# Issuing the attention inner loop of a transformer layer by pairs of key tiles, with a fourth score bank

## The reference

```python
xn = _layernorm(x)                       # x: (8, 2048, 1024)
# attention branch
c_q, c_kv = xn @ W_DQ + b_DQ, xn @ W_DKV + b_DKV          # 32 wide
q = concat([c_q @ W_UQ + b_UQ, c_q @ W_QR + b_QR])        # per head 128 + 32
k = concat([c_kv @ W_UK + b_UK, xn @ W_KR + b_KR])        # the 32-wide part is shared by the heads
v = c_kv @ W_UV + b_UV                                    # per head 128
attn = softmax(q @ k.T / sqrt(160)) @ v                   # per head, 2048 x 2048
out_a = attn @ W_O + b_O
# expert branch: gates from a few rounds of normalisation, best two of eight
g, p = relu(xn @ wg[e]), xn @ wp[e]
out_f = sum over the two best e of gate[e] * ((g * p) @ wo[e])
return x + out_a + (xn + out_f)
```

## Time and profile before

| | us |
|---|---|
| median of 3 runs | 3950.96 |
| lowest run | 3939.86 |
| the profiled execution | 3941.66 |
| its span on the slowest core (core 1) | 3940.1 |
| spans of the 8 cores | 3915.8 to 3940.1 |

### The profile page before, as it was taken

The page is one execution under the profiler, slowest core; times in us unless marked ns, Lnnn a source line. Parts: engine busy times, 40 slices in busy tenths (PEclk is TensorE's granted clock), DMA queues, the critical chain, the costliest instruction groups (busy, mean ns, idle before and its releaser), DMA issues.

```text
span 3940.1 us, 43697 instructions; the slowest of 8 cores (3915.8 to 3940.1 us)
## 1 busy us (share of the span) xinstructions
PE 3601.7 (91%) x15210; PEld 1463.8 (37%) x15210; DVE 830.0 (21%) x1274; ACT 745.0 (19%) x1211; POOL 726.7 (18%) x1038
## 2 busy tenths in 40 slices
PE   3599999999999999898989899999999999999997
PEld 1243444444344444222222222444444444444443
DVE  3321121212121121122222222212121111212121
ACT  2310101101010101244444443011010101011010
POOL 1022222222222222000000000122222222222221
PEclk8699999999999999788888879999999999999998
DMA  4178879797878879300000000487878879787876
GB/s 75 37 74 107 92 95 110 76 114 73 113 76 112 95 92 110 52 1 0 1 1 0 1 1 1 79 110 79 119 67 110 83 105 100 87 110 78 118 67 131
DMA packets 618328, 290.68 MB, mean 74 GB/s; under 512 B 547324, under 2 KB 547357, under 8 KB 618118
## 3 DMA queue, kind: packets, MB, share of 16 engines
q0 software_dynamic: 610624, 271.03, 58.9%
q1 hardware_dynamic: 7494, 16.86, 1.3%
HBM read 550.39 MB, written 8.39 MB: 142 GB/s over the span
## 4 chain that ended last, share of the span: by engine, by line
PE 84%; DVE 5%; DMA 4%; ACT 3%; issue 3%; POOL 0%; DVEq 0%; SPq 0%; ACTq 0%; POOLq 0%
PE psum L625 22%; PE psum L557 21%; PE psum L565 21%; PE psum L788 4%; PE psum L784 4%; DMA s_areaC<-wexp 3%; DVE s_resid L647 3%; PE psum L774 3%; PE psum L778 3%; PE psum L819 2%; PE psum L676 1%; ACT s_areaB L794 1%; PE psum L358 1%; ACT s_areaB L726 1%; ACT s_areaB L719 1%
## 5 line engine op out<-in xcount | busy, mean ns | idle before, releaser
L625 PE MATMUL psum<-s_areaC,s_areaA 128*128 128x512 bf16 x4096 | 944.4, 391 | 102.8 <-DVE s_resid L647 73.7
L557 PE MATMUL psum<-s_xnT,s_wgbuf 128*128 128x512 bf16 x4096 | 967.6, 379 | 20.5 <-DVE s_resid L647 16.4
L565 PE MATMUL psum<-s_xnT,s_wpbuf 128*128 128x512 bf16 x4096 | 967.6, 379 | 0.0
L576 ACT ACTIVATE s_areaB<-psum 128x512 bf16<-128x512 f32 x512 | 306.2, 598 | 2458.1 <-PE psum L557 2457.8
L521 POOL DMA_DIRECT2D s_wgbuf<-wg x256 | 224.6, 877 | 2285.0 <-PE psum L557 2213.9
L625 PEld LDWEIGHTS psum<-s_areaC,s_areaA 128*128 128x128 bf16 x4096 | 406.8, 100 | 637.8 <-issue 191.5
L583 DVE TENSOR_TENSOR s_areaA<-s_areaB,psum 128x512 bf16<-128x512 bf16 x512 | 352.2, 688 | 1351.6 <-PE psum L565 1345.7
L557 PEld LDWEIGHTS psum<-s_xnT,s_wgbuf 128*128 128x128 bf16 x4096 | 399.0, 98 | 506.8 <-issue 28.5
L565 PEld LDWEIGHTS psum<-s_xnT,s_wpbuf 128*128 128x128 bf16 x4096 | 400.8, 98 | 483.3
L606 POOL DMA_DIRECT2D s_areaC<-wexp x512 | 271.9, 539 | 678.9 <-PE psum L625 677.2
L647 DVE SCALAR_TENSOR_TENSOR s_resid<-psum,s_w_tm,s_resid 128x512 f32<-128x512 f32 x256 | 192.1, 750 | 935.4 <-PE psum L625 911.4
(11 more groups left out here) (113 smaller groups left out, 706.5 us busy)
## 6 DMA issues: line engine op xcount, KB each, us to landing
s_areaC<-wexp POOLq DMA_DIRECT2D x512, 256.0 KB, 7.9
s_wgbuf<-wg POOLq DMA_DIRECT2D x256, 256.0 KB, 4.6
s_wpbuf<-wp POOLq DMA_DIRECT2D x256, 256.0 KB, 5.7
s_resid<-x SPq DMA_DIRECT2D x16, 512.0 KB, 3.8
y<-s_resid SPq DMA_DIRECT2D x2, 4096.0 KB, 12.6
s_areaC<-wo_attn POOLq DMA_DIRECT2D x1, 2048.0 KB, 14.1
s_wcat<-wdq POOLq DMA_DIRECT2D x1, 64.0 KB, 4.0
s_wcat<-wdkv POOLq DMA_DIRECT2D x1, 64.0 KB, 4.1
```

The costliest lines, as they stand in the source:

```text
L557: w.do("tensor", lambda t, c_=c, tb_=tb, tt2_=tt2, gs_=gs, b_=gb: t.matmul(bank(b_)[:, :], S["wgbuf"].ap()[:, gs_, c_, :], S["xnT"].ap()[: ...
L565: w.do("tensor", lambda t, c_=c, tb_=tb, tt2_=tt2, gs_=gs, b_=pbk: t.matmul(bank(b_)[:, :], S["wpbuf"].ap()[:, gs_, c_, :], S["xnT"].ap()[ ...
L576: w.do("scalar", lambda s, b_=gb, sl_=gp_count % 2: s.activation(out=Ebuf[:, sl_, :], in_=bank(b_)[:, :], func=AF.Relu), inc="sS")
L625: w.do("tensor", lambda t, f_=f, dh_=dh, tt_=tt, bk_=bk, ws_=ws, tb_=tb: t.matmul(bank(bk_)[:, :], hbuf[:, f_, tt_ * 128:(tt_ + 1) * 128], ...
```

## The change

The iteration of the inner loop covers two key tiles. Iteration `t_` waits for the exponential of tile `2 t_ - 2` (the newer of the two whose output comes next is `k0 = 2 t_ - 2`, the older is `k1 = 2 t_ - 3`), issues O and Z of `k1`, O and Z of `k0`, and then S1 and S2 of the tiles `2 t_` and `2 t_ + 1`. There are 10 iterations instead of 18. The scores rotate over four banks, 0, 1, 4 and 5. Bank 4 is therefore no longer free for the broadcast of the reciprocal, which now goes into the bank of the sum it was made from (3 or 7), and no longer waits for the earlier copy out of bank 4. The broadcast is issued after iteration 3, which is after S2 of tile 7. `Ebuf` keeps its three slots.

```diff
-                h_, qb_, qg_, ob_, rectok = pend
+                h_, qb_, qg_, ob_, zb_, rectok = pend
                 w.wait("tensor", "vS", rectok)
-                w.wait("tensor", "vS", tok.get("przb_cp"))
-                w.do("tensor", lambda t: t.matmul(bank(4)[:, :], S["onesr"][:], rzv,
-                                                  start=True, stop=True), inc="tS")
+                w.do("tensor", lambda t, zb2=zb_: t.matmul(bank(zb2)[:, :], S["onesr"][:], rzv,
+                                                           start=True, stop=True), inc="tS")
...
-                w.do("vector", lambda v: v.tensor_copy(rzbv, bank(4)[:, :]), inc="vS")
+                w.do("vector", lambda v, zb2=zb_: v.tensor_copy(rzbv, bank(zb2)[:, :]), inc="vS")
...
-                    for kt in range(NT + 2):
-                        ko = kt - 2
-                        if ko >= 0:
-                            w.wait("tensor", "sS", tok[("exp_s", h, qb, ko)])
-                        if kt == 0:
+                    for t_ in range(NT // 2 + 2):
+                        k1, k0 = 2 * t_ - 3, 2 * t_ - 2
+                        if k0 >= 0:
+                            w.wait("tensor", "sS", tok[("exp_s", h, qb, min(k0, NT - 1))])
+                        if t_ == 0:
...
-                        if ko >= 0:
-                            (O and Z of tile ko)
-                        if kt < NT:
-                            b = (0, 1, 5)[kt % 3]
+                        for ko in (k1, k0):
+                            if 0 <= ko < NT:
+                                (O and Z of tile ko)
+                        for kt in (2 * t_, 2 * t_ + 1):
+                            if kt >= NT:
+                                continue
+                            b = (0, 1, 4, 5)[kt % 4]
                             (S1, S2 and the exponential of tile kt)
...
-                        if kt == 5:
+                        if t_ == 3:
                             flush_przb()
...
-                    tok["pend"] = (h, qb, qg, ob, w.tok("vS"))
+                    tok["pend"] = (h, qb, qg, ob, zb, w.tok("vS"))
```

More of the change, by code:

```diff
@@ L772, in walk @@
                             w.wait("tensor", "sS", tok.get("exp_prev_last"))
-                        if ko >= 0:
[L774 to L781, removed]
-                        if kt < NT:
-                            b = (0, 1, 5)[kt % 3]
+                        for ko in (k1, k0):
+                            if 0 <= ko < NT:
+                                w.do("tensor", lambda t, kt_=ko, ob_=ob: t.matmul(
+                                    bank(ob_)[:, :], v_h[:, kt_, :], Ebuf[:, kt_ % 3, :],
+                                    start=(kt_ == 0), stop=(kt_ == NT - 1)),
+                                    inc="tS" if ko == NT - 1 else None)
+                                w.do("tensor", lambda t, kt_=ko, zb_=zb: t.matmul(
+                                    bank(zb_)[:, :], S["onesm"][:], Ebuf[:, kt_ % 3, :],
+                                    start=(kt_ == 0), stop=(kt_ == NT - 1)),
+                                    inc="tS" if ko == NT - 1 else None)
+                        for kt in (2 * t_, 2 * t_ + 1):
+                            if kt >= NT:
+                                continue
+                            b = (0, 1, 4, 5)[kt % 4]
                             w.do("tensor", lambda t, kt_=kt, b_=b, qb_=qb: t.matmul(
```

## The result

The changed kernel takes 4010.8 us (median of 9 runs) against 3949.3 us for the kernel before (median of 10 runs): the ratio is 1.0165, with a 95% interval of 1.0146 to 1.0183. It is slower by 1.65%, or some 65 us by the ratio (the two medians lie 61.5 us apart), which is inside the 2% that the chances spoke of, and clear of the measurement's own noise. Forecast were 4003 us, with 3972 to 4035 as the range. Some executions of any 8-core kernel here are disturbed and much longer; all ratios in this document, and all means over several executions, leave them out, while the medians do not.

A forecast was written before the change was run, and what follows sets the result against it. The prediction took TensorE's own stream to set the time, with ScalarE hidden. It summed 3941.7 us (profiled execution) + 58 (blocks) + 2 (half clock) = 4002, rounded up to 4003 us; range 3972 to 4035.

The forecast's parts named there:

- The balance before: Old attention inner loop: O starts 1.30 us after its own S2, just covering the 1.29 us needed, almost no slack.
- The stall: Changed inner loop at full clock: TensorE waits 0.42 us per pair for the newer exponential; pair 2.55 us against 2.14.
- The block: Attention query block of 16 tiles at full clock: 19.31 us before, 21.12 after; +1.81 us over 32 blocks, +58 us.
- The half clock: Start of attention heads at 1.2 GHz: 142 us costing 63 before, 181 us costing 65 after, +2 us.
- The parts at nothing: Attention's four score banks, broadcast into the finished sum's bank, dropped wait and later VectorE oT copy: no cost.
- The sum: Whole kernel: profiled execution 3941.7 us plus 58 and 2 gives 4002, rounded up to 4003 us.
- rival 1: Clock falls again inside attention heads, in three blocks of four: +112 us, 4115 us, slower by over 2%; chance 0.10.
- Rival 2: Clock returns at 5 us in every attention head: -49 instead of +2, 3951 us, no change; chance 0.05.
- Rival 3: No wait in the attention pair, 2.13 us each; only the end-of-block wait changes, -13 us, 3929 us; chance 0.02.

The follow-up runs named there:

- the last run: Kernel before plus trimmed unread matmuls (384 columns in projections, extra ones before attention and after each head's last value projection), run once more: ratio 0.9893, median 3906.3 us.
- the first form: Unread 512-column matmuls added in the projections: kernel before 0.9939, changed kernel 1.0091, changed kernel with split wait 0.9939, all against the kernel before.
- the trimmed form: Unread matmuls cut to 384 columns after 512-wide projections, extra ones before attention and after value projections: split wait 0.9884 and 0.9874, old loop 0.9879 and 0.9893.

## Why the prediction was right

**The balance before: right.** The 1.29 us from S2 to its own O, against 1.30 us that the old order gave it, was the number on which the rest hung. The shorter exponential shows both sides of it: with 0.21 us less on ScalarE, the kernel before loses 10 us (13 expected from the blocks' ends), and the pair of the changed one follows one to one.

**The stall: right in place and size.** 2.55 us a pair was forecast and measured, 1.28 against 1.29 us for the release. Splitting the wait removed it, with everything else of the change in place.

**The block: 0.06 us too low.** 19.31 and 21.12 us were forecast, 1.81 apart. At clock 1.00 throughout, a head gives 77.2 / 4 = 19.3 and 84.7 / 4 = 21.2 us, 1.88 apart, so 60 us instead of 58. The interval Z to O, for which no row existed, was 0.21 us as taken (1916.35 to 1916.56). What is left is rounding: O to Z and Z to O are 0.215 us, so that the pair is 2.56, six times a block, and the tail 1.39 instead of 1.36.

**The half clock: the weakest step, and the sum of it came out near by luck.** I gave the two heads with early returns the 25 us of their neighbours and kept the other six, 181 us in all; it was 161 us on the slowest core. The reasoning that the early returns at 5 us would be lost was right in that no head of the changed kernel returned before 6 us after its start. But the returns did not gather at 25 us: they came after 7 to 8, 12, 16, 24, 30 or 34 us. The price of 0.36 us for a half-clock microsecond holds: a head with 33 us lasts 97.0 us and one at full clock 84.7, 0.37 each, and over the eight heads (735 us, about 679 at full clock) it is 0.35. The price before, 0.44, was a little high: the eight heads of core 1 last 678.5 us in the kernel before and 619.4 at full clock in the last run, 59 us for 142, or 0.42 each. So the term was 161 x 0.35 = 56, against 59 before: -3 instead of +2. That the changed loop has more half clock is shown by the executions on record (494 us a core against 471), and the prediction had that direction right. Which heads return late differs from kernel to kernel and between cores with the same code, and no experiment here settles what decides it: the kernel with the shorter exponential has 78 us on two cores and 213 on a third.

**The parts at nothing: right.** Banks and broadcast alone gave 1.0002. VectorE's later copy held up nothing: the list of waits of the changed kernel in attention has none of O or Z for VectorE.

**The sum** was 3941.7 + 60, rounded up to +61; by the ratio the change is +65, and between the two profiled executions +67. With the terms as measured, the blocks give +60 and the half clock -3, 57 in all, and the stretch forecast grew by 57.6. That the forecast of 4003 is so near 4010.8 is in part luck: the blocks' 2 us too few and the half clock's 5 us too many cancel in part, and in the profiled execution (4007.4 us of span) another 8.5 us are differences between cores in the stage before attention, and 0.9 the stage behind it, which the argument did not foresee.

**The rivals.** The clock did not fall inside a head in any of the 64 heads of the kernel after, so rival 1 did not occur, although TensorE waits in every pair. The Trainium skill (TensorE: Matmul & The Clock Gate, "A second HAM failure mode: psum-queue depth-cycling"), which says that short idle times between groups of matmuls can make the clock swing, is not borne out by these stalls of 0.42 us in 2.55. Falls deep inside a head do exist: in the split wait with added matmuls, on two cores in each of two executions, the clock fell 27 to 37 us after the first head's start. That loop does not have the stalls, and what brings these falls on stays open. Rival 2, an early return in all heads, did not come either (two cores of the kernel with the shorter exponential came near it, with 8 us in all heads but the first); with the half clock taken away from both kernels the 60 us stay. Rival 3 is refuted by the timeline. The prediction also said that waits would rise "to about 200, of 0.2 to 0.3 us"; they rose to 187, of 0.26 us on average.

## What to carry to other kernels

When work of two ages is grouped in one iteration of an in-order engine, each part needs the wait for its own input: one wait for the newest input ahead of the group holds back work whose data is ready, and the slack that hid the producer's latency shrinks by the length of that work (here from 1.30 to 0.87 us, against 1.29 needed). Before such an edit, add up the producer's whole latency from the start-to-start times, and set it against what the consumer issues between the production and the wait; ScalarE's busy share of 45% in attention (372 of 821 us) said nothing of this. Matmuls whose result nobody reads, put where TensorE waits for other engines, can be worth more than a shorter loop: here 1.1 to 1.3% of the measured time, against 0.3% (11 us) that the split wait saves in the traces and that the measured time does not show.

## What the runs showed of the hardware

The granted clock is at 0.50 in a head's projections, in which TensorE issues one 32-row matmul per 0.78 us, and it stayed there for 5 to 34 us after dense matmuls had begun, in both loops; a microsecond of it costs 0.42 us in the old loop and 0.35 in the changed one, averaged over a core's heads. With the added matmuls in the gaps it remained at 1.00 through the projections and the whole of 140 of the 168 second to eighth heads in the three kernels with the first form of them, and of 223 of 224 in the four executions with the trimmed form. I had not expected that the return could take so long with TensorE issuing without a gap, nor that it would be so uneven: in one execution of one kernel, heads of the same code had 5 us and 28 us. This spread, up to 12 us a head, is larger than what the stalls cost (7.5 us a head) or the split wait saves (1.5 us), and it is why the time of this 8-core kernel, which is that of its slowest core, could not show the 11 us that the traces show.
